# Decoder recurrence: a half-height alignment table on two row groups, and two changes of order around the alignment

## The reference

```python
enc_proj = jnp.einsum('btd,ad->bta', hbatch, Wa_h)
def step(carry, tgt):
    s, c, alpha = carry
    f = lax.conv_general_dilated(alpha, conv_w, (1,), 'SAME', ...)
    e = jnp.einsum('a,bta->bt', va, jnp.tanh(enc_proj + (s @ Wa_s.T)[:, None, :]
                                             + jnp.einsum('bft,af->bta', f, Wa_f) + ba))
    e = jnp.where(mask, e, jnp.float32(-1e+30))
    alpha_new = jax.nn.softmax(e, axis=1)[:, None, :]
    g = jnp.einsum('bt,btd->bd', alpha_new[:, 0], hbatch)
    y = jnp.tanh(g @ L_gy_w.T + L_gy_b + s @ L_sy.T) @ L_yy_w.T + L_yy_b
    rec = tgt @ L_ys.T + s @ L_ss.T + g @ L_gs_w.T + L_gs_b
    ig, fg, cg, og = jnp.split(rec, 4, axis=1)
    c_next = _sig(fg) * c + _sig(ig) * jnp.tanh(cg)
    s_next = _sig(og) * jnp.tanh(c_next)
    return ((s_next, c_next, alpha_new), y)
```

## Time and profile before

| | us |
|---|---|
| median of 3 runs | 4053.48 (4051.23 to 4054.08) |
| profiled execution | 4058.55 |
| its span | 4056.8 |
| TensorE matmuls busy | 3261.3 (80%) |
| VectorE busy | 2232.7 (55%) |
| ScalarE busy | 1577.2 (39%) |
| TensorE idle before the filter matmuls (L1789), 82.9 of it ended by the table's DMA | 84.9 |

### The profile page before, as it was taken

How to read it: one execution, slowest core, us unless ns; L and a number is a source line. 1 busy time by engine, 2 the same in 40 slices (tenths; PEclk the granted TensorE clock), 3 DMA queues, 4 the chain that set the end, 5 groups by cost and what they waited for, 6 DMA issues and landing times. The chain is left out here.

```text
span 4056.8 us, 109059 instructions
## 1 busy us (share of the span) xinstructions
PE 3261.3 (80%) x43050; PEld 2192.1 (54%) x43122; DVE 2232.7 (55%) x5373; ACT 1577.2 (39%) x3966; POOL 505.4 (12%) x1854
## 2 busy tenths in 40 slices
PE   7556568544489999998598999999999999965998
PEld 4424145322266666666354666666666666623554
DVE  2656767588845555555213555555555555563444
ACT  2221134344422222222112666666666666622222
POOL 0000421233300000000000000000000000033222
PEclk8576689877789999999798999999999999975888
DMA  2000020200010000000101333333333333301000
GB/s 95 3 3 0 10 46 9 86 0 0 0 44 0 0 0 0 0 0 0 52 26 50 90 90 90 90 90 88 91 89 90 90 90 87 93 18 48 25 26 31
DMA packets 278734, 176.56 MB, mean 44 GB/s; under 512 B 14320, under 2 KB 267840, under 8 KB 278608
## 3 DMA queue, kind: packets, MB, share of 16 engines
q1 hardware_dynamic: 275920, 172.57, 14.5%
q0 software_dynamic: 2752, 3.18, 0.5%
HBM read 164.98 MB, written 13.90 MB: 44 GB/s over the span
## 5 line engine op out<-in xcount | busy, mean ns | idle before, releaser
L1828 PE MATMUL ps<-de_hg,st_at 128*32 128x128 f32 x16384 | 516.3, 275 | 0.3 <-DVE st_at L1990 0.3
L1828 PEld LDWEIGHTS ps<-de_hg,st_at 128*32 128x32 f32 x16384 | 424.5, 110 | 31.6 <-DVE st_at L1990 0.5
L1893 ACT ACTIVATE st_th<-ps,st_sw 128x128 f32<-128x128 f32 x1024 | 292.8, 369 | 248.0 <-PE ps L1800 248.0
L1973 DVE TENSOR_TENSOR st_th<-ps,st_sw 128x512 f32<-128x512 f32 x256 | 177.2, 692 | 155.1 <-PE ps L1800 155.1
L1247 PEld LDWEIGHTS ps<-sa_xt,w_wq 128*128 128x128 f32 x2048 | 234.7, 194 | 11.1 <-issue 9.3
L1247 PE MATMUL ps<-sa_xt,w_wq 128*128 128x128 f32 x2048 | 237.9, 278 | 2.0 <-ACT sa_xt L1363 2.0
L1766 POOL COPY de_ah<-st_at 128x8 f32 (+1 forms) x256 | 51.1, 199 | 1507.0 <-DVE st_at L1990 1507.0
L1318 PE MATMUL ps<-sa_wo,sa_ct 128*128 128x512 f32 x512 | 225.0, 598 | 13.1 <-issue 13.1
L1789 PE MATMUL ps<-st_hk,st_cwt 112*32 112x128 f32 x4096 | 164.7, 278 | 84.9 <-DMA st_hk<-padded_alignments 82.9
L2228 PE MATMUL ps<-rf_wb,rf_sp 128*128 128x512 bf16 x737 | 202.2, 434 | 4.7 <-issue 2.9
L1800 PE MATMUL ps<-st_fs,st_waf 32*128 32x128 f32 x4096 | 186.5, 296 | 12.2
(11 more groups left out here) (410 smaller groups left out, 6456.5 us busy)
## 6 DMA issues: line engine op xcount, KB each, us to landing
st_hk<-padded_alignments SPq DMA_DIRECT2D x254, 448.0 KB, 3.6
X<-in_x_dram SPq DMA_DIRECT2D x16, 512.0 KB, 9.2
out_dram<-X SPq DMA_DIRECT2D x16, 512.0 KB, 2.7
w_wq<-in_Wq_perm_dram SPq DMA_DIRECT2D x1, 4096.0 KB
sa_wo<-in_Wo_perm_dram SPq DMA_DIRECT2D x1, 4096.0 KB, 14.2
gate_inputs<-dp_ro SPq DMA_DIRECT2D x16, 256.0 KB, 2.3
st_rin<-gate_inputs SPq DMA_DIRECT2D x128, 32.0 KB, 3.3
rf_wf<-in_weightT_dram SPq DMA_DIRECT2D x8, 512.0 KB, 4.3
```

What stands on the lines that cost most here:

```text
L1828: ins = pe.matmul(R[g][32 * q:32 * q + 32, :], at[g][:, b, :], hg[:, BG * g + b, q * P:(q + 1) * P], start=False, stop=(b == BG - 1), tile ...
L1893: ins = act.activation(th[g][:, b, :], sums(g, 0)[:, b // 2, (b % 2) * P:(b % 2 + 1) * P], ACT.Tanh, bias=sw[g][:, b:b + 1])
L1973: dve.tensor_tensor(th[g][:, 4:8, :].rearrange("p (k s) n -> p k s n", s=2), sums(g, 1).rearrange("p k (s n) -> p k s n", s=2), sw[g][:, 4 ...
```

## The change

The table keeps one row for two taps: row r of a group of 64 rows holds elements from 2r on, 129 of them, so that the even tap reads columns 0 to 127 and the odd tap columns 1 to 128 of the same row. Even-numbered sequences go to partitions 0 to 63, odd-numbered ones to partitions 64 to 127, with one DMA each. The taps are laid out alike in `cwt` (now 128 taps, 27 of them zero). `filter_rows` is 16 matmuls of 64 rows: for each tap parity, for each of the two row groups, for each of the four column groups. The two row groups write two PSUM banks, `fs` has two planes of 128 columns, and the other PSUM tiles move bank to make room.

On TensorE a half now begins with the wait for `al`, then the state term, then the turn of the alignment. On VectorE `align` is cut in two: `invert` (the reciprocal) stays in its place, and `align` goes behind the state. ScalarE's `keep_filters` waits for the reciprocal and no longer for `al`. TensorE adds 1 to a semaphore behind its wait for the table.

```diff
-TAPSA, PADA = 112, 50
+TAPSA, PADA = 128, 50
-            hk = pair("hk", [TAPSA, BG, P])
+            hk = pair("hk", [P, BG // 2, P + 4])
-            fs = pair("fs", [P, P])
+            fs = pair("fs", [P, 2, P])
-            R = [ps[:, 4 + g, 0:P] for g in range(G5)]
-            T = [ps[:, 4 + g, P:2 * P] for g in range(G5)]
-            F = [ps[:, 4 + g, 2 * P:3 * P] for g in range(G5)]
-            E = [ps[:, 6 + g, 0:P] for g in range(G5)]
-            AT = [ps[:, 6 + g, P:2 * P] for g in range(G5)]
-            SW = [ps[:, 6 + g, 3 * P:3 * P + BG] for g in range(G5)]
+            R = [ps[:, 4 + 2 * g, 0:P] for g in range(G5)]
+            T = [ps[:, 4 + 2 * g, P:2 * P] for g in range(G5)]
+            F = [ps[:, 4 + 2 * g:6 + 2 * g, 2 * P:3 * P] for g in range(G5)]
+            E = [ps[:, 5 + 2 * g, 0:P] for g in range(G5)]
+            AT = [ps[:, 5 + 2 * g, P:2 * P] for g in range(G5)]
+            SW = [ps[:, 7 - 2 * g, 3 * P:3 * P + BG] for g in range(G5)]
-            def hankel(g):
-                return bass.AP(pad_d, g * BG * AW, [[1, TAPSA], [AW, BG], [1, P]])
+            def hankel(g, r):
+                return bass.AP(pad_d, (g * BG + r) * AW, [[2, 64], [2 * AW, BG // 2], [1, P + 1]])
                     for i in range(2):
-                        sp.dma_start(cwt[:, i, 16 * i:16 * i + 10], a["conv_wT"]).then_inc(w_load, 16)
+                        for s in range(2):
+                            sp.dma_start(cwt[64 * i:64 * i + 64, s, 16 * i:16 * i + 10],
+                                         a["conv_wT"].rearrange("(t s) c -> s t c", s=2)[s]).then_inc(w_load, 16)
...
-                        sp.dma_start(hk[o][:, :, :], hankel(o)).then_inc(hk_in[o], 16)
+                        for r in range(2):
+                            sp.dma_start(hk[o][64 * r:64 * r + 64, :, 0:P + 1], hankel(o, r)).then_inc(hk_in[o], 16)
...
-                            pe.wait_ge(hk_in[g], 16 * n)
-                        for i in range(2):
-                            for j in range(4):
-                                ins = pe.matmul(F[g][32 * j:32 * j + 32, :], cwt[:, i, :], hk[g][:, 2 * j + i, :],
-                                                start=(i == 0), stop=(i == 1), tile_position=(0, 32 * j), skip_group_check=True)
+                            pe.wait_ge(hk_in[g], 32 * n)
+                            pe.sem_inc(windows_seen)
+                        for s in range(2):
+                            for r in range(2):
+                                for j in range(4):
+                                    ins = pe.matmul(F[g][32 * j:32 * j + 32, r, :], cwt[64 * r:64 * r + 64, s, :],
+                                                    hk[g][64 * r:64 * r + 64, j, s:s + P], start=(s == 0), stop=(s == 1),
+                                                    tile_position=(64 * r, 32 * j), skip_group_check=True)
...
-                                                fs[g][32 * j:32 * j + 32, :], start=False, stop=True,
+                                                fs[g][32 * j:32 * j + 32, i, :], start=False, stop=True,
...
                     def turn_alignment(g, n):
-                        pe.wait_ge(al_ready[g], n + 1)
                         pe.transpose(AT[g], al[g][:, :], ident[:, :]).then_inc(at_ps[g], 1)
                     def half(g, n, o, m, u, more):
                         front = not isinstance(m, int) or m <= LAST
+                        pe.wait_ge(al_ready[g], n + 1)
+                        if front:
+                            state_term(o, m)
                         turn_alignment(g, n)
                         if front:
-                            state_term(o, m)
                             spread_filters(o, m)
...
-                            act.wait_ge(al_ready[g], n)
-                        act.activation(fs[g][:, :], F[g], ACT.Identity, scale=ri[g][:, 0:1]).then_inc(f_kept[g], 1)
+                            act.wait_ge(ri_ready[g], n)
+                        act.activation(fs[g][:, :, :], F[g], ACT.Identity, scale=ri[g][:, 0:1]).then_inc(f_kept[g], 1)
...
-                    def align(link, g, n):
+                    def invert(g, n):
                         dve.wait_ge(exp_done[g], n + 1)
-                        link(dve.reciprocal(ri[g][:, :], sm[g][:, :]))
+                        dve.reciprocal(ri[g][:, :], sm[g][:, :]).then_inc(ri_ready[g], 1)
+
+                    def align(g, n):
+                        dve.wait_ge(ri_ready[g], n + 1)
                         dve.tensor_scalar(al[g][:, :], ex[g][:, :], ri[g][:, 0:1], None, ALU.mult).then_inc(al_ready[g], 1)
...
                         if front:
-                            align(link, o, m)
+                            invert(o, m)
                         dve.wait_ge(tc_done[g], n + 1)
                         if more:
                             dve.wait_ge(hist_s[g], n + 1)
                             dve.scalar_tensor_tensor(out=states(g), in0=to, scalar=1.0, in1=tc[g][:, :], op0=ALU.add,
                                                      op1=ALU.mult).then_inc(st_ready[g], 1)
+                        if front:
+                            align(o, m)
```

More of the change, by code:

```diff
@@ L1643, in stage_decoder @@
             vas = t3.sb("vas", [P, 2, 32])
-            cwt = t3.sb("cwt", [TAPSA, 2, 32])
+            cwt = t3.sb("cwt", [P, 2, 32])
             waf = t3.sb("waf", [P, 2, P])
@@ L1671, in psems @@
                 return [t3.sem(f"{name}{g}") for g in range(G5)]
-            w_load, set_up, dve_seq, pad_out, cleared = t3.sems("w_load set_up dve_seq pad_out cleared")
+            w_load, set_up, dve_seq, pad_out, cleared, windows_seen = t3.sems("w_load set_up dve_seq pad_out cleared windows_seen")
             (at_ps, at_ready, r_sum, rec_ready, t_ps, gates_done, cc_done, tc_done, st_ready, sw_ps, sw_ready, filled0, filled1,
-             f_ps, f_kept, conv_ps, added, th_done, e_ps, e_max, exp_done, al_ready, ex_out, hk_in, rin_in, hist_a, hist_s) = (
+             f_ps, f_kept, conv_ps, added, th_done, e_ps, e_max, exp_done, ri_ready, al_ready, ex_out, hk_in, rin_in, hist_a, hist_s) = (
                 psems(n) for n in "at_ps at_ready r_sum rec_ready t_ps gates_done cc_done tc_done st_ready sw_ps sw_ready filled0 filled1 "
-                "f_ps f_kept conv_ps added th_done e_ps e_max exp_done al_ready ex_out hk_in rin_in hist_a hist_s".split())
-            R = [ps[:, 4 + g, 0:P] for g in range(G5)]
-            T = [ps[:, 4 + g, P:2 * P] for g in range(G5)]
-            F = [ps[:, 4 + g, 2 * P:3 * P] for g in range(G5)]
-            E = [ps[:, 6 + g, 0:P] for g in range(G5)]
-            AT = [ps[:, 6 + g, P:2 * P] for g in range(G5)]
-            SW = [ps[:, 6 + g, 3 * P:3 * P + BG] for g in range(G5)]
-            SETUP, LOADS = 23, 16 * (5 + 10)
+                "f_ps f_kept conv_ps added th_done e_ps e_max exp_done ri_ready al_ready ex_out hk_in rin_in hist_a hist_s".split())
+            R = [ps[:, 4 + 2 * g, 0:P] for g in range(G5)]
[4 more added lines that the diff above has]
+            SW = [ps[:, 7 - 2 * g, 3 * P:3 * P + BG] for g in range(G5)]
+            SETUP, LOADS = 23, 16 * (5 + 12)
             filled = [filled0, filled1]
-            def hankel(g):
-                return bass.AP(pad_d, g * BG * AW, [[1, TAPSA], [AW, BG], [1, P]])
+            def hankel(g, r):
+                return bass.AP(pad_d, (g * BG + r) * AW, [[2, 64], [2 * AW, BG // 2], [1, P + 1]])
             def diag(v):
@@ L2029, in _ @@
                     fill(1, 0)
-                    link = Chain(dve, dve_seq)
                     top(0, 0)
-                    align(link, 0, 0)
+                    invert(0, 0)
+                    align(0, 0)
                     def start(it):
                         state["it"] = it
-                        state["link"] = Chain(dve, dve_seq, 1 + it * 2 * U5 * 3)
+                        state["link"] = Chain(dve, dve_seq, it * 2 * U5 * 2)
                     steps(dve, half, start)
```

## The result

The changed kernel takes 4107.8 us (median of 4 runs, 4105.1 to 4112.2) against 4052.4 for the kernel before beside it: a ratio of 1.0137, 95% interval 1.012 to 1.0155. The forecast was 4062 with a range to 4094: slower, as it said, but by 55 us and not by 8.

What follows compares the result with a forecast made beforehand. TensorE was taken as held by waits for the table's DMA and VectorE's `al`, in alternating halves. Halves of 5.31 + 0.08 = 5.39 against 5.362 give +7.8 us, plus 0.6 setup: +8.4, median 4062, range 4041 to 4094.

Steps and rivals of the forecast that it cites:

- State 0.03 behind `tc`: VectorE in each half: the state starts 0.03 us after ScalarE's `tc` ends, 0.04 earlier than today.
- `al` 0.08: VectorE: `al`, now behind the state, starts 0.08 us after the state's start and takes 0.29.
- spread at S+0.48: TensorE: S is the half's turn of the alignment; with the state term first the spread starts at S+0.48 against 0.40, +0.08.
- the row groups don't overlap: Rival, filter matmuls: 16 more records cost +0.40 us, 0.28 covered, +31 us in all, 4093; chance 0.07.
- `fs` 0.47 for 0.46: `fs` from two banks: 256 instead of 128 columns takes 0.46 us, +0.09, inside the filters' slack of 0.28.
- Table transfer: Table DMA in the loop: second of two issued about 0.35 us later, landing 2.4 after issue; DMA wait and echo gone.
- The point of decision: Table DMA: the landing decides the half's length only from 3.5 us up; at the expected 2.4 it does not.
- 7.31 plus the landing: One group's cycle per step, filters through second table issue: 7.31 us plus the landing, against two halves of 5.39, 10.78.
- the chain: Loop path through state, `al` and turn: 5.31 us a half plus 0.08 for the late spread, 5.39 against 5.362.
- the transfer doesn't get shorter: Rival, table DMA: second lands in 3.7 us, cycle 11.01 a step against 10.72, +37 us, 4091; chance 0.05.
- one more gap on the new chain: Rival, TensorE's turn with two waits starts later behind `al`: 0.05 to 0.12 us more per half, 4075 to 4093; chance 0.12.
- In setup: Ahead of the loop: two more small loads, 0.3 us each on the queue, +0.6 us in all.

Runs made afterwards that it cites:

- orders_only: Kernel before with both new orders (VectorE, TensorE) and `fs` waiting for the reciprocal, old table in one DMA: 4070.2 us against 4060.6 for the kernel before.
- table_only: Changed kernel with both old orders, new table kept, `SW` in another bank (values off by 0.036, for time alone): 4100.7 us against 4060.6 for the kernel before.

## Why the prediction was right and wrong

**Right.** That the orders cost time, and most of their terms. State 0.03 behind `tc`, `al` 0.08 (0.09) behind that, spread at S+0.48 (2746.53 to 2747.01), the eight filter tiles at once at no cost (0.67 for 32 records, so the 0.40 of the rival "the row groups don't overlap" did not come), `fs` 0.47 for 0.46. The sign of the whole is right for the reason given: the orders alone make the loop slower. One agreement is luck. orders_only came out 9.6 us above the kernel before beside it, where the sum was 8.4; but its loop is 0.075 x 256 = 19 us longer, and stages with the same code gave 10 back.

**Wrong: the transfer.** The failing step is "*Table transfer*": "the second is issued about 0.35 later" and "I take 3.6 - 1.7 + 0.5 = 2.4". Measured: issue 0.61, second issue 0.65 later, landing 3.1. 0.65 + 3.1 = 3.75 from the first issue by medians (3.68 in the mean), where one DMA took 3.6 to 3.7. So with little more than half of the bytes the last of the table lands no earlier. The 2.4 is what such bytes take on 48 to 80 partitions (2.2 to 2.5) and not on 64. The point of decision in the prediction was a landing of 3.5 with the second issue 0.35 behind; 3.1 at 0.65, with the store's 0.04, stands at 3.44 on that scale, just short of it.

**Wrong: the path from the landing to the filters was put at nothing.** The cycle ends with "7.31 plus the landing". The runs show 0.13 more from the last landing to the first filter matmul, and 0.10 for the 0.05 from the filters to `fs`. With these two the landing decides from 3.3 up and not from 3.5, and 3.44 is above that: the table's cycle is 10.98 (table_only), above the 10.87 of the chain. The kernel before could have told. The same sum for it, 0.65 + 0.05 + 0.37 + 0.05 + 2.57 + 1.52 + 1.66 + 3.6 = 10.47, is 0.25 short of its 2 x 5.362 = 10.72. Most of the gap is the 0.16 from its landing to its filters. The rival "the transfer doesn't get shorter" had 0.05; in its effect it was the case, for each transfer did get shorter (3.1 for 3.6) and the pair did not. Its 11.01 a step is close to the measured 11.04 by luck: it had 4.05 from the first issue to the last landing, for 3.68, and nothing behind it. The issue could have been seen too: the earlier trace rows had the issue of the table at 0.31 and that of a store of 4 KB at 0.57. Issue time does not follow bytes, and I took the small one for a form that no row showed.

**Wrong: one gap.** The rival "one more gap on the new chain" came true in one half of two: 0.13 and not 0.05 behind `al`, where an ALU_OP carries the wait. The mean chain is 5.437 and not 5.39: 12 us of the 47 missing.

**Missing from the sum.** I added one bound's excess to the other's nothing: with the chain at 5.44 and the cycle close to it (5.49), the two together come out at 5.437 + 0.085 = 5.522, above either. That 0.085 is 22 us. That it comes about because late transfers add to a chain that is itself close is my reading; only its size is shown. In setup, 2.8 us and not 0.6. The 11 us that are left of the 47 lie in stages with the same code and between the single profiled executions and the medians; no run takes them apart.

## What to carry to other kernels

Fewer bytes make a small transfer shorter only if its form stays fast: split in two, its parts pay the issue twice, and the second lands a full landing after its own issue, so time the new form (issue and landing, by itself) before building on it. Where two chains stand within a few per cent of each other, undoing or shortening one shows nothing; take one out of the way entirely (here by leaving a DMA out, or by a faster form) to see the price of the other. Two changes of order that cost 0.075 us a half beside a wait cost 0.25 as soon as the wait was gone. And add up the cycle of the kernel as it is before adding up that of the change: where the sum falls short of the measured length, a term is missing from both.

## What the runs showed of the hardware

Not expected: a DMA onto 64 neighbouring partitions takes 0.57 us to issue and 3.0 to land with 129 KB, and one onto 80 takes 0.30 and 2.5 with 160 KB. The landing is counted from the issue's start and has the issue in it. With 256 KB, 64 neighbours take 3.7, every second partition 3.0, and 128 partitions 3.1. Two row groups of 64 on four column groups run as eight tiles at once: 32 records in 0.67 us, 16 on four tiles in 0.65. From the last landing of a table to the matmul that waited for it, it is 0.09 to 0.14 us in 214 of 254 steps of table_only. And the same wait costs TensorE 0.05 us on the matmul's own load and 0.12 to 0.13 on an instruction ahead of it, which can be the arithmetic for the next wait.
